# Attention and SwiGLU on one core: three batches' outputs moved into middle groups, gate and up one group ahead

## What is computed

```python
q = (xn @ Wq.T + bq).reshape(b, t, 16, 8)      # 16 heads of 8
k, v = ...                                     # 4 heads of 8, each shared by 4 query heads
q, k = rope(q), rope(k)
probs = softmax(q k^T / sqrt(8))               # over all 1024 positions
attention = (probs v).reshape(b, t, 128) @ Wo.T + bo
ffn = (silu(xn @ wg.T) * (xn @ wu.T)) @ wd.T   # 384 hidden, weights are integers / 127
```

## Time and profile before

| | us |
|---|---|
| median of 3 runs | 772.57 (772.14 to 774.59) |
| the profiled execution | 775.68 |
| its span | 773.9 |
| busy in the span: PE | 722.5 (93%) |
| DVE | 692.7 (90%) |
| ACT | 618.1 (80%) |
| POOL | 223.5 (29%) |
| mean granted clock of PE | 0.985 |

### The profile page before, as it was taken

One profiled execution on the slowest core, in us unless ns is written; L12 is line 12 of the kernel. 1 busy time (PEld: TensorE's weight loads), 2 busy tenths in 40 slices (PEclk: granted clock), 3 DMA queues, 4 the chain that ended last, 5 costly groups with the idle time before them and its releaser, 6 DMA issues.

```text
span 773.9 us, 13580 instructions
## 1 busy us (share of the span) xinstructions
PE 722.5 (93%) x4856; PEld 213.2 (28%) x4856; DVE 692.7 (90%) x1284; ACT 618.1 (80%) x1267; POOL 223.5 (29%) x364
## 2 busy tenths in 40 slices
PE   3598999999999999999999999999999999999996
PEld 1222222222222222222222222222222222222352
DVE  6787999999999999999999999999999999999731
ACT  1534979888888988888888989798888889898864
POOL 3408647373830302122030303021120303021110
PEclk9787999999999999999999999999999999999999
DMA  7511123131221101011111101011111111010021
GB/s 220 140 34 32 40 76 113 33 113 33 75 71 32 32 1 54 10 31 33 32 32 32 32 22 42 1 33 32 32 32 33 32 33 32 2 32 2 2 70 40
DMA packets 29323, 34.34 MB, mean 44 GB/s; under 512 B 5545, under 2 KB 20137, under 8 KB 29129
## 3 DMA queue, kind: packets, MB, share of 16 engines
q1 hardware_dynamic: 26472, 26.23, 12.2%
q0 software_dynamic: 1920, 5.12, 2.2%
q10 hardware_dynamic: 864, 2.15, 0.8%
HBM read 23.12 MB, written 9.96 MB: 43 GB/s over the span
## 4 chain that ended last, share of the span: by engine, by line
PE 74%; DVE 15%; ACT 5%; DMA 2%; issue 2%; SPq 1%; ACTq 0%; DVEq 0%
PE acc_ps L953 29%; PE banks L867 18%; DVE mx L719 13%; PE banks L884 11%; PE banks L958 8%; ACT probs L560 5%; PE banks L972 3%; PE banks L964 2%; DMA y_all<-in_x 1%; PE banks L837 1%; PE banks L989 1%; PE banks L843 1%; DMA k_rows<-part 1%; DVE y_all L766 1%; PE banks L980 0%
## 5 line engine op out<-in xcount | busy, mean ns | idle before, releaser
L719 DVE TENSOR_REDUCE mx<-banks 128x1 f32<-128x512 f32 x1024 | 637.9, 684 | 38.1 <-PE banks L867 36.0
L560 ACT ACTIVATE probs<-banks 128x512 f32<-128x512 f32 x1024 | 549.4, 604 | 101.9 <-PE banks L884 97.8
L884 PE MATMUL banks<-qc,kc 51*128 51x512 bf16 x1024 | 305.6, 384 | 15.6 <-ACT probs L560 10.6
L867 PE MATMUL banks<-ka,qa 48*128 48x512 bf16 x1024 | 300.6, 386 | 11.1 <-DVE mx L719 6.1
L953 PE MATMUL acc_ps<-probs,v_grp 128*32 128x512 f32 x2048 | 273.4, 606 | 0.0
L867 PEld LDWEIGHTS banks<-ka,qa 48*128 48x128 bf16 x1024 | 68.7, 94 | 303.4 <-DVE mx L719 235.5
L447 POOL TENSOR_TENSOR neg_max<-row_max,nought 128x16 bf16<-128x16 f32 x31 | 6.9, 222 | 295.4 <-DVE row_max L725 295.4
L884 PEld LDWEIGHTS banks<-qc,kc 51*128 51x128 bf16 x1024 | 66.0, 94 | 55.1 <-ACT probs L560 52.3
L958 PE MATMUL banks<-xn_T,w_ffn 128*128 128x256 f32 x192 | 67.5, 433 | 0.0
L953 PEld LDWEIGHTS acc_ps<-probs,v_grp 128*32 128x32 f32 x2048 | 40.4, 108 | 81.2 <-ACT probs L560 51.1
L491 POOL TENSOR_TENSOR gated<-gu 128x256 f32<-128x256 f32 x48 | 35.2, 733 | 53.4 <-ACT gu L617 53.4
(11 more groups left out here) (86 smaller groups left out, 310.1 us busy)
## 6 DMA issues: line engine op xcount, KB each, us to landing
qa<-q_rows SPq DMA_DIRECT2D x32, 192.0 KB, 3.4
qc<-q_rows SPq DMA_DIRECT2D x64, 96.0 KB, 2.7
q_rows<-part POOLq DMA_DIRECT2D x18, 256.0 KB, 4.3
ka<-k_rows SPq DMA_DIRECT2D x32, 96.0 KB, 2.2
kc<-k_rows SPq DMA_DIRECT2D x32, 96.0 KB, 2.2
y_all<-in_x SPq DMA_DIRECT2D x4, 512.0 KB, 11.5
out<-y_all SPq DMA_DIRECT2D x8, 256.0 KB, 2.3
k_rows<-part SPq DMA_DIRECT2D x6, 192.0 KB
```

Of the source, the lines that this page charges most:

```text
L560: nc.scalar.activation(probs[:, s % SLOTS, j, :], banks[:, score_bank(G * s + j), :], ACT.Exp, scale=SCALE).then_inc(exp_done, 1)
L719: nc.vector.tensor_reduce(out=mx[:, h, col, k:k + 1], in_=ps, op=ALU.max, axis=AX.X).then_inc(max_done, 1)
L867: nc.tensor.matmul(ps, qa[par][rows, j // 2, t * P:(t + 1) * P], ka[par][rows, k * W:(k + 1) * W], start=True, stop=True).then_inc(a_ready, 1)
L884: nc.tensor.matmul(banks[:, score_bank(u), :], kc[par][rows, kt * P:(kt + 1) * P], qc[par][rows, h, j // 2, :], start=True, stop=True).the ...
```

## The change

- Three batches' outputs (u = 0 to 5, two halves each) move to groups 5, 6, 9, 10, 13 and 14: STAGE in step 9, PROJ in steps 12 and 14. The half batch u = 6 gets the same steps of the last group, and u = 7 stays behind its end. A PROJ is now half of one: two tiles, 256 columns, and so are its addition and its store.
- ACT, not DVE, copies a STAGE to `ctx_T`.
- GATE and UP of chunk g + 1 run in group g (steps 3, 4, 6, 7, 10, 11), DOWN of chunk g in steps 1 and 2 of group g. The last group has no GATE or UP. Those of chunk 0 run in the prologue: PE makes all six ahead of its wait for `qa_loaded`, in the three banks of the first units, and ACT and POOL work on them there.
- POOL's order: chunk 0's `hidden` and the bias come ahead of the first copies of values; in a group, `hidden(g+1, 0)` and `(g+1, 1)` stand before `split_max(g+1, 0)`, `hidden(g+1, 2)` behind it and ahead of `later`. DVE waits only for the bias of its own batch.
- Orders now differ in length from group to group, so banks are counted through (`ring_slots`).

```diff
-JOB_AT = {1: (GATE, 0), 2: (UP, 0), 3: (GATE, 1), 4: (UP, 1), 5: (NEG_T, 1), 6: (GATE, 2), 7: (UP, 2), 8: (CTX, 0),
-          10: (DOWN, 0), 11: (DOWN, 1), 13: (NEG_T, 0), 16: (CTX, 1)}
-MIDDLE = (GATE, UP, DOWN)
-OUT_AT = (4, 5, 6, 7, 8, 9, 12)
+JOB_AT = {1: (DOWN, 0), 2: (DOWN, 1), 3: (GATE, 0), 4: (UP, 0), 5: (NEG_T, 1), 6: (GATE, 1), 7: (UP, 1), 8: (CTX, 0),
+          10: (GATE, 2), 11: (UP, 2), 13: (NEG_T, 0), 16: (CTX, 1)}
+FOR_NEXT = ((GATE, 0), (UP, 0), (GATE, 1), (UP, 1), (GATE, 2), (UP, 2), (NEG_T, 0))
+MIDDLE = (GATE, UP, DOWN, PROJ)
+def output_steps(u):
+    return {9: (STAGE, u), 12: (PROJ, 2 * u), 14: (PROJ, 2 * u + 1)}
+OUT_AT = {KV * (b + 1) + 1 + h: output_steps(2 * b + h) for b in range(B - 1) for h in range(2)}
+OUT_AT[NG - 1] = output_steps(OUTS - 2)
...
+def step_order(g, s):
+    units = [(MAX, n) for n in range(PER * s + LEAD, PER * (s + 1) + LEAD) if g < NG - 1 or n < AU]
+    jobs = [JOB_AT[s]] if s in JOB_AT and (g < NG - 1 or JOB_AT[s] not in FOR_NEXT) else []
+    jobs += [OUT_AT[g][s]] if g in OUT_AT and s in OUT_AT[g] else []
...
+        order += [JOB_AT[STEPS], (STAGE, OUTS - 1), (PROJ, 2 * OUTS - 2), (PROJ, 2 * OUTS - 1)]
...
 @block: SP
-            for u in range(OUTS):
+            for u in range(2 * OUTS):
...
 @block: POOL
+            for c in range(FC):
+                hidden(0, c)
+            pool.wait_ge(xn_done, 2)
+            pool.wait_ge(xn_done_act, 1)
+            for b in range(B):
...
             def group(g, par):
                 split_max(g, 1)
-                for c in range(FC):
-                    hidden(g, c)
                 if g + 1 < NG:
+                    hidden(g + 1, 0)
+                    hidden(g + 1, 1)
                     split_max(g + 1, 0)
+                    hidden(g + 1, 2)
                 if g + 1 < B:
                     later(g + 1)
...
 @block: ACT
+            def copy_ctx_T(u, ps):
+                if u > 1:
+                    act.wait_ge(o_ps, 2 * (u - 1))
+                act.wait_ge(ctx_T_ps, u + 1)
+                nc.scalar.activation(ctx_T[:, (u % 2) * W:(u % 2 + 1) * W], ps, ACT.Copy).then_inc(ctx_T_done, 1)
...
             copy_later(1, 1)
+            for c in range(FC):
+                act.wait_ge(ffn_up, 2 * (c + 1))
+                nc.scalar.activation(th[:, c, :], first_bank(c)[:, 0:CH], ACT.Tanh, scale=0.5).then_inc(gu_done, 1)
+                nc.scalar.activation(gu[:, c, :], first_bank(c), ACT.Copy).then_inc(gu_done, 2)
...
 @block: DVE
-                dve.wait_ge(bo_added, B)
+                dve.wait_ge(bo_added, g // KV + 1)
...
-                piece = y_all[:, u * HT:(u + 1) * HT, :]
-                nc.vector.tensor_tensor(piece, piece, ps.rearrange("p (t d) -> p t d", d=D),
+                piece = y_all[:, u * HT // 2:(u + 1) * HT // 2, :]
+                nc.vector.tensor_tensor(piece, piece, ps[:, 0:HW].rearrange("p (t d) -> p t d", d=D),
...
 @block: PE
+            pe.wait_ge(w_done, 1)
+            for c in range(FC):
+                for n in range(2):
+                    ffn_in(0, n, c, first_bank(c)[:, n * CH:(n + 1) * CH])
             pe.wait_ge(qa_loaded[0], DMAS)
             for a in range(LEAD):
+                if a < FC:
+                    pe.wait_ge(gu_done, 3 * (a + 1))
...
-                pe.wait_ge(ctx_T_done, u + 1)
-                for t in range(HT):
-                    c = (u % 2) * W + t * P
+                pe.wait_ge(ctx_T_done, u // 2 + 1)
+                for t in range(HT // 2):
+                    c = u % 4 * HW + t * P
```

More of the change, by code:

```diff
@@ L32 @@
 STEPS = NH * NT
+HW = W // 2
 SLOTS = 2
@@ L93, in step_order, with group_order @@
     n = ahead(jobs)
     return units[:n] + jobs + units[n:]
[L97 to L100, removed]
+def group_order(g):
+    if g < 0:
+        return [(MAX, AU + LEAD + i) for i in range(PER)]
+    order = [o for s in range(1, STEPS + (g < NG - 1)) for o in step_order(g, s)]
+    if g == NG - 1:
+        order += [JOB_AT[STEPS], (STAGE, OUTS - 1), (PROJ, 2 * OUTS - 2), (PROJ, 2 * OUTS - 1)]
+    return order
@@ L103, in unit, with ring_slots @@
+def ring_slots(g):
+    return sum(len(group_order(k)) for k in range(g))
 def unit(a):
@@ L462, in copy_v @@
                 nc.gpsimd.tensor_copy(v_grp[par][:, :, 0:HD], v_all[:, :, g, :]).then_inc(v_grp_done, 1)
[L464 to L483, removed]
             def hidden(g, c):
@@ L496, in hidden, with later @@
                 nc.gpsimd.tensor_tensor(hid[:, c, :], th[:, c, :], gated[:, c, :], ALU.add).then_inc(hid_done, 1)
+            for c in range(FC):
[3 more added lines that the diff above has]
+            for b in range(B):
+                nc.gpsimd.tensor_tensor(y_all[:, b * NT:(b + 1) * NT, :], y_all[:, b * NT:(b + 1) * NT, :],
+                                        bo_sb[:, :].unsqueeze(1).to_broadcast([P, NT, D]),
+                                        ALU.add).then_inc(bo_added, 1)
+            pool.wait_ge(ones_done, 2)
+            pool.wait_ge(v_done, 1)
+            copy_v(0, 0)
+            copy_v(1, 1)
+            pool.wait_ge(neg_step, NEG)
+            split_later(0)
+            def later(b):
+                split_later(b)
+                for i, (_, n) in enumerate(BLOCKS):
+                    pool.dma_start(q_rows[b * KV:(b + 1) * KV, :, i, :, :].rearrange("g j d t -> (g j) d t"),
+                                   part[:, (b + 1) % 2, n, :]).then_inc(q_dma, 16)
+                pool.wait_ge(q_dma, BLOCK_DMAS * b)
+                pool.sem_inc(q_stored, 2)
             def group(g, par):
                 split_max(g, 1)
-                for c in range(FC):
-                    hidden(g, c)
                 if g + 1 < NG:
+                    hidden(g + 1, 0)
+                    hidden(g + 1, 1)
                     split_max(g + 1, 0)
+                    hidden(g + 1, 2)
                 if g + 1 < B:
@@ L620, in group @@
                             copy_neg(g + 1 - n, n, bank(slot))
+                        if kind == STAGE:
+                            copy_ctx_T(n, bank(slot))
                         slot += 1
@@ L626, in group @@
                         nc.scalar.activation(acc_sb[:, s // NT, :], acc_ps[:, :], ACT.Copy).then_inc(acc_copied, 1)
+                if left == 1:
+                    copy_ctx_T(OUTS - 1, bank(slot + 1))
             exps(0, 1, range(G))
@@ L798, in group @@
             def group(g, order):
-                for slot, (kind, n) in enumerate(order):
+                for slot, (kind, n) in enumerate(order, ring_slots(g)):
                     if kind == MAX:
@@ L807, in _ @@
             for g in range(NG):
-                group(g, ORDER if g < NG - 1 else LAST_ORDER)
+                group(g, group_order(g))
         @block.tensor
@@ L1010, in bank_left, with take @@
                     pe.wait_ge(o_done, n + 1)
-            def take(g, par, slot, order):
+            def take(g, par, slot, order, before):
                 if slot >= RING:
@@ L1016, in take @@
                 else:
-                    bank_left(g, *ORDER[slot - RING], back=1)
+                    bank_left(g - 1, *before[slot - RING])
                 kind, n = order[slot]
-                ps = bank(slot)
+                ps = bank(ring_slots(g) + slot)
                 if kind == MAX:
@@ L1048, in group @@
             def group(g, pair, par, left):
-                order = LAST_ORDER if left == 1 else ORDER
+                order, before = group_order(g), group_order(g - 1)
                 slot = 0
@@ L1071, in group @@
                             for _ in range(len(todo) - len(units)):
-                                take(g, par, slot, order)
+                                take(g, par, slot, order, before)
                                 slot += 1
                         if units:
-                            take(g, par, slot, order)
+                            take(g, par, slot, order, before)
                             slot += 1
```

56 lines of the change are left out of this document (21 added, 35 removed).

## The result

| | before | after |
|---|---|---|
| median, us | 774.73 (772.14 to 776.86, 20 runs) | 778.99 (774.06 to 782.79, 20 runs) |
| ratio to before | | 1.005, 95% interval 1.0035 to 1.0064 |
| profiled execution, us | 775.68 | 775.77 |
| its span | 773.9 | 773.7 |

What follows compares the result with a forecast made beforehand. In middle groups PE was taken to bound steps with a job, DVE's maxima most without. Terms summed to +3.7 us (span 773.9 to 777.6); +3.6 on a median of 772.6 gave 776.2, 8-in-10 range 770.0 to 779.5.

Steps and rivals of the forecast that it cites:

- last group: Last group: gate, up and most outputs leave it, so it takes 40.1 us against 46.10, -6.0.
- tail: End of the kernel: last addition and store half as big, -0.4 us (-0.7 to 0).
- outputs in six groups: Groups 5, 6, 9, 10, 13, 14: STAGE +0.15, step 12's PROJ +0.35, step 14's 0; +3.0 us in all.
- order of the jobs: Middle groups: moving down to steps 1 and 2, with gate and up in its place, costs 0.
- POOL's queue: Groups 1 to 3, step 5: one more `hidden` delays POOL's split and PE waits, +5.1 us (3 to 5.5).
- prologue: Start: six gate and up matmuls ahead of the first maximum, -0.5 us; +2.6 if they run at half clock.
- clock in the stalls: Behind PE's stalls in groups 1 to 3: half clock, half the full price taken, +2.5 us (0 to 5.1).
- Rival 3: Last group: PE's clock falls in its thin steps, +3.5 on the forecast, 779.7 us; chance 0.16 together with another rival.
- Rival 2: Groups 1 to 3: POOL's delay is absorbed, no stall, -3.9, 768.7 us; chance 0.15.
- Rival 1: Groups 1 to 3: PE stalls but loses no clock, +1.2, 773.8 us; chance 0.27.

Runs made afterwards that it cites:

- e1: The changed kernel, but POOL waits for the DMAs of `later` behind the next group's split: 770.35 us, 0.994 of the kernel before.
- e3: The changed kernel with two spare matmuls where PE waits for POOL in step 5 of groups 1 to 3: 772.60 us, ratio 0.9985.
- Experiments 1, 2 and 6: Experiment 1 is e1 (770.35 us), experiment 2 is e2 (786.21 us), experiment 6 is f4 (774.50 us).
- f2: The kernel of e1 with the STAGE copies on DVE again instead of ACT: 769.71 us.
- e4: The changed kernel with chunk 0's six gate and up matmuls behind PE's wait for `qa_loaded`: 783.80 us, ratio 1.0128.
- e2: The kernel before with three spare multiplications (2.3 us) on POOL ahead of `later` in groups 0 to 2: 786.21 us, ratio 1.0146.
- f1: The kernel of e1 with the three batches' outputs put back into the last group: 771.76 us.
- f3: The kernel of e1 with one spare matmul ahead of each of the last six maxima of the prologue: 770.64 us.
- g2: The kernel of e1 with both halves of PROJ in step 14, step 12 without a job: 770.55 us.
- f4: The kernel before with the one edit of e1: 774.50 us, ratio 1.0001.
- g1: The kernel of e2 with two spare matmuls where PE waits in step 5 of groups 1 to 3: 779.99 us, ratio 1.0061.

## Why the prediction was right, point by point

Forecast +3.6 us and 776.2; measured +4.3 and 778.99, in the range of 770.0 to 779.5, on the side that had 0.54. The base explains most of the 2.8 us by which 776.2 is short: the kernel before has 774.73 over 20 runs and had 772.57 over the three that the forecast stood on (+2.2). The sum is nearer than its parts, and that is luck: the terms without the clock came out 1.2 us lower than forecast (0.0 for +1.2), the clock higher.

| term | forecast | measured | where |
|---|---|---|---|
| last group | -6.0 | -6.3 | 46.10 to 39.81 |
| tail | -0.4 | -0.6 | 8.25 to 7.68 |
| outputs in six groups | +3.0 | +2.5 | 21.08 to 21.49, six times |
| order of the jobs | 0 | 0 | 43.02 in both |
| POOL's queue | +5.1 | +5.4 | 1.84, 2.03, 1.51 |
| prologue | -0.5 | -1.0 usually, -2.9 in the profiled execution | first copies of the context; 73.72 to 70.86 |
| clock in the stalls | +2.5 | +3.0 to +5.9 | e1 and e3; at most 3.6 by the mean clock |

The sum closes with these terms: -6.3 - 0.6 + 2.5 + 5.4 - 1.0 (the usual gain of the prologue, below) is 0.0, and the mean moved by +4.0 (774.60 to 778.62; the medians by +4.3). Of that 0.6 lie outside the span, which no run here explains, and the 3.4 that are left fit what the runs give for the clock. A remainder is no measurement of it.

- **POOL's queue** was read right to a tenth in groups 1 and 3: a `hidden` of 2.30 us, less the 0.48 by which PE itself comes later, where the kernel before had the split ready as it was wanted. In group 2 POOL came 0.2 later still. Experiments 1, 2 and 6 show it from three sides.
- **The outputs.** The addition of 256 columns takes this, and DVE goes on without a gap behind it, in step 12 as in step 14:

```profile
327.73 0.41 DVE L812 TENSOR_TENSOR y_all<-y_all,banks 128x256 f32<-128x256 f32 x1
328.06 4.96 DVE L751 TENSOR_REDUCE mx<-banks 128x1 f32<-128x512 f32 x8
332.94 0.41 DVE L812 TENSOR_TENSOR y_all<-y_all,banks 128x256 f32<-128x256 f32 x1
333.27 1.28 DVE L751 TENSOR_REDUCE mx<-banks 128x1 f32<-128x512 f32 x2
334.71 2.48 DVE L751 TENSOR_REDUCE mx<-banks 128x1 f32<-128x512 f32 x4 [0.16 <-PE banks L893]
```

  DVE's idle time in step 14 shrank from 0.49 to 0.16, so that addition was free, as predicted; the one in step 12 is the 0.33 that was paid. STAGE cost less than its 0.15. f2 shows that the step isn't as strictly DVE's as I had it.
- **The clock** is the term that was mis-sized. I took half of the full price of three falls, at 1.7 each. Both halves of that were low. Of the nine stalls in three traces (the changed kernel's, e4's and e2's) six were followed by half clock, one, two and three of three. And a fall cost 1.6 only twice; it cost 2.9 three times in e2 and 3.1 once in e4. Even the 3.0 of experiment 1 is over the 2.5 that I took, though within what the runs can tell. The rule of the Trainium skill that I weighed (TensorE: Matmul & The Clock Gate, "Why this matters for your kernels"), which warns only of longer gaps, would have had no loss here; the runs decide against it for this kernel: waits of 1.66 to 2.22 us in dense work were followed by half clock, and filling them took 6 us off two medians.
- **The prologue.** The six take 2.86 and not up to 4.2, so PE is not late for qa, and the profiled execution gained 2.9. But the first copy of the context came at 93.3 there, and at 95.4, 91.1, 92.6, 94.2, 94.4 and 91.9 in kernels with the same prologue (e1, e3, f2, f1, f3 with its spare matmuls, g2); with the old prologue at 95.7, 93.3, 93.2 and 94.8 (before, f4, e2, g1). The means are 93.3 and 94.3, so a usual gain is about 1 us, and with this scatter the forecast of 0.5 can't be told from it. e4 shows what the placing is worth: the first weighing comes 5.1 us later, and the median is 4.8 higher, if the six stand one line lower.
- **Rival 3**, half clock in the thin last group, fell: the last group's granted clock was 1.00 in every trace. **Rival 2** fell with the row at 131.14. **Rival 1** describes the profiled execution nearly (one fall of three), but not the median.

What stays open is the rest of the spread: with no stall and the same code, executions of e1 differ by 6 us (767.4 to 773.3), with a mean granted clock of 0.991 in the two shortest and 0.987 in the two longest. The first copy of the context, at 91.1 to 95.4 with this prologue, varies by more than half of that, so much of it seems to arise in the start; which waits there decide was not settled (f3). The tail adds to it: it had a clock of 1.00 in both profiled executions, but 0.68, 0.71 and 0.84 in e2, f4 and g1, 0.85 and 0.89 in e3 and f2. In e2 and f4, which have the old tail, the last projection then took 2.04 and 1.96 us instead of 1.13, and the tail 9.13 and 9.06 instead of 8.25. So the -0.6 of the tail is a difference of two undisturbed executions.

## What to carry to other kernels

An engine that is busy 29% of the time can still be the one that decides: look in its written order for the place where a long piece of work ends just when another engine wants what stands behind it, and move the wait for a DMA behind that. A stall of TensorE in dense work can cost more than itself: here stalls of 1.7 to 2.3 us cost 1.5 to 4.8, by chance from one execution to the next. Test it with matmuls that do nothing. Where a change adds stalls, one profiled execution can hide the loss; compare the spread and the clock of many executions.

## What the hardware showed that I had not expected

- Waits of 1.74 to 1.93 us between dense matmuls were followed by half clock in three of three cases (e2: 0.87 over each half of 26.2 us), and cost 2.9 us more than themselves. In the changed kernel's trace it followed the wait of 2.22 us and not those of 2.03 and 1.70; in e4's it followed those of 2.00 and 1.66 and not that of 2.29.
- In the prologue PE came back to full clock within the six matmuls of e4 (4.42 us), where in the kernel before pairs of maxima with four transpositions between them (36.8 to 40.2) stayed at 0.50 with PE busy throughout. The same pairs with eight projections (L843) between them, from 46.0 to 50.0, had 1.00 with PE busy throughout.
- The last group, with PE busy 35.58 of 39.81 us by its rows and one weighing in 2.45 us, kept 1.00, while the tail behind it, with PE waiting 0.8 us three times, did not in five of twelve traces.
